# Delta-rule layers of a hybrid network: the inverse of a 32-token triangle in full, then one solution step

## The reference, cut to what matters

```python
def step(W, inp):
    qt, kt, vt, bt = inp
    wk = jnp.einsum('bhde,bhe->bhd', W, kt)
    v_new = bt * (vt - wk)
    W = W + jnp.einsum('bhd,bhe->bhde', v_new, kt)
    out = jnp.einsum('bhde,bhe->bhd', W, qt)
    return (W, out)
# q, k = softmax over 32; beta = sigmoid; the input is a layer norm's output times slow_w
```

## Time and profile before

| | us |
|---|---|
| three runs, median (lowest, highest) | 5387.88 (5385.71, 5416.66) |
| the profiled execution | 5345.09 |
| its span, first to last instruction | 5343.3 |
| first delta-rule stage, start of M's scaling in chunk 0 to chunk 31 | 392.9 to 1194.3 |
| second delta-rule stage, the same | 1638.8 to 2453.3 |

### The profile page before, as it was taken

The page is one execution under the profiler, slowest core; times in us unless marked ns, Lnnn a source line. Parts: engine busy times, 40 slices in busy tenths (PEclk is TensorE's granted clock), DMA queues, the critical chain, the costliest instruction groups (busy, mean ns, idle before and its releaser), DMA issues. The chain is left out here.

```text
span 5343.3 us, 141254 instructions
## 1 busy us (share of the span) xinstructions
PE 4536.1 (85%) x57740; PEld 2868.5 (54%) x57741; DVE 2973.0 (56%) x5849; ACT 2153.1 (40%) x4123; POOL 853.9 (16%) x2139
## 2 busy tenths in 40 slices
PE   3678888888988988998777987799999999985995
PEld 1247777773437777774354654345454455443663
DVE  3445444453024444454577887488685885864343
ACT  1123232332123333231365566177575775741221
POOL 0000000000000000000454555011111111102112
PEclk7779888898988888798888988899999999996997
DMA  1000000000000000000100000000000000005223
GB/s 42 2 7 3 3 3 3 3 3 18 0 6 3 3 3 3 3 3 3 38 1 1 1 1 1 10 1 0 1 0 1 1 0 1 0 3 194 87 85 100
DMA packets 47557, 85.79 MB, mean 16 GB/s; under 512 B 7120, under 2 KB 38128, under 8 KB 46064
## 3 DMA queue, kind: packets, MB, share of 16 engines
q1 hardware_dynamic: 40944, 61.84, 3.4%
q0 software_dynamic: 6144, 16.79, 1.0%
HBM read 45.05 MB, written 33.55 MB: 15 GB/s over the span
## 5 line engine op out<-in xcount | busy, mean ns | idle before, releaser
L1769 PE MATMUL psum<-hm_ex,hm_mix 128*128 128x512 f32 x1024 | 510.9, 622 | 42.1 <-ACT hm_Aq L1849 38.1
L1835 ACT ACTIVATE hm_ex<-psum,hm_nm 128x1024 f32<-128x1024 f32 x256 | 285.5, 1115 | 300.6 <-DVE hm_nm L1893 300.6
L1769 PEld LDWEIGHTS psum<-hm_ex,hm_mix 128*128 128x128 f32 x1024 | 175.7, 191 | 353.1 <-issue 345.4
L1908 DVE COPY hm_A<-psum 128x1024 f32<-128x1024 f32 x256 | 312.9, 1222 | 51.5 <-PE psum L1778 47.8
L1903 DVE TENSOR_SCALAR_CACHE_REDUCE hm_plus<-hm_Aq,hm_cbcol,hm_sums 128x1024 f32<-128x1024 f32 x256 | 340.5, 1330 | 0.0
L1893 DVE TENSOR_REDUCE hm_nm<-psum 128x1 f32<-128x1024 f32 x256 | 311.1, 1215 | 14.5 <-PE psum L1757 14.5
L1778 PEld LDWEIGHTS psum<-K,hm_Aq 128*128 128x128 f32 x2048 | 236.7, 140 | 149.9 <-issue 145.2
L957 DVE TENSOR_TENSOR fw_M<-fw_M,psum 128x256 f32<-128x256 f32 x256 | 107.9, 421 | 344.9 <-PE psum L728 342.4
L1307 ACT ACTIVATE pt_signs<-pt_acts,pt_tb 128x1024 f32<-128x1024 f32 (+1 forms) x224 | 227.8, 1020 | 146.7 <-POOL pt_tb L1180 104.4
L1840 ACT ACTIVATE hm_junk<-hm_Aq 128x1024 f32<-128x1024 f32 x256 | 270.6, 1057 | 30.3
L1757 PE MATMUL psum<-hm_kt,hm_qd 64*32 64x512 f32 x4096 | 280.9, 607 | 0.0
(11 more groups left out here) (380 smaller groups left out, 9117.4 us busy)
## 6 DMA issues: line engine op xcount, KB each, us to landing
ex_rows_in<-ex_zero SPq DMA_DIRECT2D x2, 5120.0 KB, 24.8
ex_xs<-ex_rows_in SPq DMA_DIRECT2D x80, 128.0 KB, 2.0
ex_rows_out<-ex_ys SPq DMA_DIRECT2D x80, 128.0 KB, 1.7
ex_w<-in_ex_w SPq DMA_DIRECT2D x2, 4096.0 KB, 23.0
X<-in_x SPq DMA_DIRECT2D x2, 2048.0 KB, 12.5
out_y<-X SPq DMA_DIRECT2D x2, 2048.0 KB, 9.0
ff_w<-in_ff_w SPq DMA_DIRECT2D x2, 1024.0 KB, 5.9
pt_w_proc<-in_pt_proc SPq DMA_DIRECT2D x1, 2048.0 KB, 7.6
```

The source lines that it names most:

```text
L1769: mm = pe.matmul(bank[4 + c], mix[:, u, :], ex[:, u, 512 * c:512 * c + 512], start=True, stop=True)
L1835: act.activation(ex[:, u, :], flat2(psum[:, 2 * u:2 * u + 2, :]), ACT.Exp, bias=nm[:, u:u + 1], accum_out=rsum[:, u:u + 1]).then_inc(s_ex, 1)
L1908: dve.tensor_copy(A[:, :, :, QT_ * t:QT_ * t + QT_], flat2(psum[:, 6:8, :]).rearrange("p (m g n) -> p m g n", m=MT, g=HEADS)).then_inc(s_a ...
```

## The change

The inverse of the 32 x 32 triangle is made in full by small-tile products, and one solve with it takes the place of four. With nn = -N and nn' = -N^T (both are now made), nn^2 by a product, nz = nn z3 by another, S = 1 + nn + nn^2 on VectorE (`series`), S nz by a third, and inv = z3 + S nz (`inverse`). TensorE calls product ten times for a chunk: l8, z1, z2, tt as before; zt (the transpose of z3, as a product with the identity), and two for N and N^T, in a row behind turn; two (nb) for nn^2 and nn z3 behind gram 0; one (nc) for S nz behind through_state 1. One solve(sa) is left, behind through_state 2. VectorE's two additions `solution` become `series` (two operations of 256 columns) and `inverse` (one); `solved` now copies where it added, and stands ahead of softmax. ScalarE no longer copies r0 (512 columns) and spreads one matrix, invx, in place of two; it copies nz, zn (256 columns each) and nn (512). GpSimd clears one wide matrix in place of two.

```diff
@@ tensor
-                def product(left, right):
+                def product(b, at, left, right, sig):
                     for n in range(HEADS):
-                        for b in range(4):
-                            mm = pe.matmul(bank[5][rows(b), DH * n:DH * n + DH], right[rows(b), n, :], left[rows(b), n, :],
-                                           start=True, stop=True)
-                    mm.then_inc(s_t, 1)
-
-                def solve(by, of, sig):
+                        for c in range(4):
+                            mm = pe.matmul(bank[b][rows(c), at + DH * n:at + DH * n + DH], right[rows(c), n, :],
+                                           left(rows(c), n), start=True, stop=True)
+                    mm.then_inc(sig, 1)
...
+                def solve(a):
                     for n in range(HEADS):
-                        mm = pe.matmul(bank[2][:, 64 * n:64 * n + 64], by[:, n, :], of(n), start=True, stop=True)
-                    mm.then_inc(sig, 1)
+                        hd = DH * (2 * (n % 4) + n // 4)
+                        mm = pe.matmul(bank[2][:, 64 * n:64 * n + 64], invx[:, n, :], rhs[:, a % 2, :, hd:hd + DH],
+                                       start=True, stop=True)
+                    mm.then_inc(s_ap, 1)
...
-                    if so:
-                        pe.wait_ge(s_zx, s + 1)
-                        solve(z3x, given, s_y)
                     if ch:
                         pe.wait_ge(s_trc, i + 1)
                         pe.sem_inc(s_go, 1)
                         gram(a, 0, s_ga)
+                    if so:
+                        pe.wait_ge(s_nn, s + 1)
+                        pe.wait_ge(s_zn, s + 1)
+                        pe.sem_inc(s_go, 1)
+                        product(5, 0, of(nn[:, 0]), nn[:, 1], s_nb)
+                        product(2, C, of(zn), nn[:, 0], s_nb)
...
-                    if so:
-                        pe.wait_ge(s_nt, s + 1)
-                        pe.wait_ge(s_r0, s + 1)
-                        solve(ntx, first, s_ap)
                     if rc:
                         pe.wait_ge(s_m, r * 5 + 2)
                         through_state(ra, 1)
+                    if so:
+                        pe.wait_ge(s_s1, s + 1)
+                        pe.wait_ge(s_nz, s + 1)
+                        pe.sem_inc(s_go, 1)
+                        product(2, 0, of(s1), nz, s_nc)
...
-                    if so:
-                        pe.wait_ge(s_rk, s * 2 + 1)
-                        solve(ntx, later, s_ap)
...
                         through_state(ra, 2)
+                    if so:
+                        pe.wait_ge(s_ix, s + 1)
+                        solve(sa)
...
-                    if so:
-                        pe.wait_ge(s_rk, s * 2 + 2)
-                        solve(ntx, later, s_ap)
...
+                    if nxt:
+                        turn(i + 1, (a + 1) % 4)
                     if ch:
                         pe.wait_ge(s_z, i * 2 + 2)
                         pe.wait_ge(s_lo, i + 1)
                         pe.sem_inc(s_go, 1)
-                        product(z3, loff)
-                    if nxt:
-                        turn(i + 1, (a + 1) % 4)
+                        product(2, 0, one, z3, s_zt)
+                        product(5, 0, of(z3), loff, s_na)
+                        product(5, C, of(loff), z3, s_na)
@@ scalar
                     if so:
-                        act.wait_ge(s_y, s + 1)
+                        act.wait_ge(s_nb, s * 2 + 2)
+                        act.activation(flat(nz[:, :, :]), bank[2][:, C:2 * C], ACT.Copy).then_inc(s_nz, 1)
...
+                    if so:
+                        act.wait_ge(s_inv, s + 1)
                         if since(s, 1):
-                            act.wait_ge(s_pu, s)
-                        act.activation(r0[:, :, :, :].rearrange("p n y e -> p (n y e)"), bank[2], ACT.Copy).then_inc(s_r0, 1)
+                            act.wait_ge(s_ap, s)
+                        spread(invx, inv, 1.0, s_ix)
...
-                    if ch:
-                        act.wait_ge(s_z, i * 2 + 2)
-                        spread(z3x, z3, 1.0, s_zx)
-                        act.wait_ge(s_t, i * 5 + 5)
-                        spread(ntx, bank[5][:, 0:C].rearrange("p (h j) -> p h j", j=DH), -1.0, s_nt)
...
+                    if ch:
+                        act.wait_ge(s_zt, i + 1)
+                        act.activation(flat(zn[:, :, :]), bank[2][:, 0:C], ACT.Copy).then_inc(s_zn, 1)
+                        act.wait_ge(s_na, i * 2 + 2)
+                        act.activation(nn[:, :, :, :].rearrange("p y h j -> p (y h j)"), bank[5], ACT.Copy,
+                                       scale=-1.0).then_inc(s_nn, 1)
@@ vector
-                def solution(s, it):
-                    dve.wait_ge(s_ap, s * 3 + it + 1)
-                    dve.tensor_tensor(rk[:, :, :, :].rearrange("p n y e -> p (n y e)"), bank[2],
-                                      r0[:, :, :, :].rearrange("p n y e -> p (n y e)"), ALU.add).then_inc(s_rk, 1)
+                def series(s):
+
+                    dve.wait_ge(s_nb, s * 2 + 1)
+                    own.done(dve.tensor_tensor(s1[:, :, :], result(5), nn[:, 0], ALU.add))
+                    dve.tensor_tensor(s1[:, :, :], s1[:, :, :], small(2, HEADS), ALU.add).then_inc(s_s1, 1)
+
+                def inverse(s):
+                    dve.wait_ge(s_nc, s + 1)
+                    if since(s, 1):
+                        dve.wait_ge(s_ix, s)
+                    dve.tensor_tensor(inv[:, :, :], result(2), z3[:, :, :], ALU.add).then_inc(s_inv, 1)
...
```

More of the change, by code:

```diff
@@ L601, in fast_weight_stage @@
         compact = lambda n: sb(n, [P, HEADS, DH])
[L602 to L605, removed]
+        l8, l8t, bg, loff, qm, z1, z2, tt, z3, l2, zn, nz, s1, inv = (
+            compact(n) for n in "l8 l8t bg loff qm z1 z2 tt z3 l2 zn nz s1 inv".split())
+        nn = sb("nn", [P, 2, HEADS, DH])
+        invx = sb("invx", [P, HEADS, P])
         pu = sb("pu", [P, 2, C]); pk = sb("pk", [P, C]); pkt = sb("pkt", [P, 2, C])
@@ L610, in fast_weight_stage @@
         M = sb("M", [P, 2, P])
[L611 to L612 removed]
+        names = ("w zero staged proj dif exp qk tr trc ga gb bg l8 qm lo in t l2 tt z na zt nn zn nb s1 nz nc inv ix "
+                 "ap pu pt ptc ra u rm m intra fin go dch").split()
         (s_w, s_zero, s_staged, s_proj, s_dif, s_exp, s_qk, s_tr, s_trc, s_ga, s_gb, s_bg, s_l8, s_qm, s_lo, s_in,
[L614 removed]
+         s_t, s_l2, s_tt, s_z, s_na, s_zt, s_nn, s_zn, s_nb, s_s1, s_nz, s_nc, s_inv, s_ix, s_ap, s_pu, s_pt, s_ptc,
          s_ra, s_u, s_rm, s_m, s_intra, s_fin, s_go, s_dch) = (k.sem(f"s_{n_}_{n}") for n in names)
@@ L653, in body @@
                         if since(i, 1):
-                            pool.wait_ge(s_t, i * 5)
+                            pool.wait_ge(s_na, i * 2)
                         pool.tensor_tensor(loff[:, :, :], bg[:, :, :], off, ALU.mult).then_inc(s_lo, 1)
-                for to in (z3x, ntx):
-                    pool.memset(to[:, :, :], 0.0).then_inc(s_zero, 1)
+                pool.memset(invx[:, :, :], 0.0).then_inc(s_zero, 1)
                 for a in range(4):
@@ L775, in body @@
                         pe.sem_inc(s_go, 1)
-                        product(l8, l8t)
+                        product(5, 0, of(l8), l8t, s_t)
                     if rc:
@@ L790, in body @@
                         pe.sem_inc(s_go, 1)
-                        product(z1, l2)
+                        product(5, 0, of(z1), l2, s_t)
                     if rc:
@@ L797, in body @@
                         pe.sem_inc(s_go, 1)
-                        product(z2, l2)
+                        product(5, 0, of(z2), l2, s_t)
                     if rc:
@@ L808, in body @@
                         pe.sem_inc(s_go, 1)
-                        product(tt, l2)
+                        product(5, 0, of(tt), l2, s_t)
                     if rc:
@@ L859, in body @@
                     if ch:
-                        act.wait_ge(s_t, i * 5 + 3)
+                        act.wait_ge(s_t, i * 4 + 3)
                         act.activation(flat(tt[:, :, :]), bank[5][:, 0:C], ACT.Copy).then_inc(s_tt, 1)
@@ L886, in _ @@
                 k.load_table(act, ACT.Exp)
-                act.wait_ge(s_zero, 6)
+                act.wait_ge(s_zero, 5)
                 k.credit(act, s_fin, 1)
@@ L969, in solved @@
                     got = bank[2].rearrange("p (b m y e) -> p b m y e", b=2, m=4, y=2)
-                    was = r0[:, :, :, :].rearrange("p (b m) y e -> p b m y e", b=2)
                     for n, to in enumerate((pu[:, a % 2, :], pk[:, :])):
-                        own.mark(dve.tensor_tensor(to.rearrange("p (m b e) -> p b m e", m=4, b=2),
-                                                   got[:, :, :, n, :], was[:, :, :, n, :], ALU.add))
+                        own.mark(dve.tensor_copy(to.rearrange("p (m b e) -> p b m e", m=4, b=2), got[:, :, :, n, :]))
```

(16 more changed lines are left out.)

16 lines of the change are left out of this document (7 added, 9 removed).

## The result

The changed kernel takes 5739.31 us (median of 4 runs, 5733.02 to 5749.65), the kernel before 5396.8 (5385.71 to 5416.66) in the same job, that is, among the runs made together with it: ratio 1.0637, 95% interval 1.0598 to 1.0675. It is slower by 342 us; the forecast was +262, inside its range.

The account below looks back on a forecast made before the run. TensorE's list bounds the kernel now; after the change, instruction packet delivery would. Chunk 27.8 plus clock 2.5 gives 30.3 us a step against 26.06, +262 us over 62 steps, so 5650 us from 5387.88; range 5430 to 5870.

Parts of the forecast that it names:

- Rival A: TensorE's instruction supply: several packets fetched at once under steady demand, so delivery keeps pace; 5310 us, chance 0.12.
- B: TensorE's instruction supply: short only now and then, 1 us of stalls a chunk; 5400 us, no difference, chance 0.10.
- C: TensorE's granted clock in the stages: it does not come back; 5950 us, chance 0.10.
- chunks at full clock of 26 to 28 us: Sign expected in the profile after: how long chunks of the two stages take at full clock.
- The work, -2.3 us: TensorE's work a chunk: three solves go, -6.0 us, five products come, +3.7; net -2.3 us.
- The walk, 21.9 us against 22.4: Engines' lists through one chunk, full clock, instructions at will: 21.9 us against 22.4, two new waits included.
- 25.6 of delivery: Instruction packets a chunk: 1792 records are 7.5 packets, 25.6 us at 3.4 each, the chunk's new floor.
- 1.5 of pauses: During project and the solve, few records are used and delivery pauses: 1.5 us a chunk (0.8 to 2).
- 0.7 for the jump: Loop's jump back: stays at 3.5 us, six times in 31 steps, 0.7 us a step.
- 2.5 for the clock: TensorE's granted clock in the stages: costs 2.5 us a step, taken between 1.6 (as now) and 3.7.
- The upper value for the clock, 3.7: Upper end of the clock's cost in the stages: 3.7 us a step, half of the way to 35.
- the densest 14 us hold well over 1000 records: Sign against the forecast in TensorE's densest stretch; before the change no more than 985 were found in 14 us.

Follow-up runs that it names:

- e1: Changed kernel with six second-level products as 128-column matmuls, 1216 records a chunk, values altered: stages 1548.8 us against 1968.8; whole 9643.26 us on another path.
- e2: Kernel before with each of its five products issued twice in 32-column matmuls, +640 records a chunk: 5914.55 us, ratio 1.1073.
- e3: Kernel before with each of its five products' columns streamed once more in 128-column matmuls, +160 records a chunk: 5425.99 us, ratio 1.0159.
- e4: Changed kernel with four idle 512-column matmuls added a chunk, 16 records in all: 5732.29 us, ratio 1.0732.
- e8: e6 with the pair moved behind gram 1, nc behind with_state 1, and series and inverse later on VectorE: 5282.16 us, ratio 0.9874.
- e6: e5 with the two nb products also paired into one of 64 columns a matmul, 1408 records a chunk: 5376.77 us, ratio 0.9966.
- e5: Changed kernel without zt and the second na product, VectorE transposing z3 and nn instead, 1536 records a chunk: 5498.71 us, ratio 1.0197.
- e7: Changed kernel with only the two nb products moved, behind with_state 0 and gram 1, same records: 5704.27 us, ratio 1.065.
- e10: Kernel before with its three solves on ntx for one head only, values altered: stages 1637.6 us against 1615.9; whole 9772.39 us on another path.

## Why the prediction was right, and where its terms were off

*The bound.* It said that the chunk's floor becomes the delivery of instructions, 7.5 packets, and that taking work off does not lower it. Measured: 7.5 packets a chunk in the loop, 7.26 a step over a stage, and steps of 31.05 and 32.46 us against 30.3. e1 shows that without the extra records the loss is gone, e2 against e3 that records slow the kernel before as well, at equal columns, and the packets' times that the pauses end when one has landed. Rival A (delivery keeps pace, 5310) falls with e1; B (short now and then, 5400) with 5.2 us of "issue" a step. C (the clock does not come back, 5950) is not wholly gone: its number is off by 210 us, and a clock that never came back would be granted at 0.5 and not at 0.71 and 0.68, but no chunk ran at full clock, where the kernel before had 29 that did. For the same reason the sign "chunks at full clock of 26 to 28 us" could not be read.

*The work, -2.3 us.* The prices held at full clock: a product 0.74, the solve 2.00; and a copy out of PSUM in `solved` takes 0.42 (0.41 was taken), as do the operations of `series` and `inverse` (418 to 425 ns). Not all of VectorE's operations of 256 columns do: M's scaling (L1005) takes 0.35, two in `lower` 0.53 (L950) and 0.84 (L951). Busy time nonetheless rose by 0.65 us a step, as it was done at 0.71 and 0.68 in place of 0.89 and 0.85.

*The walk, 21.9 us against 22.4.* Both new waits came: l8 by up to 1.2 us (22 times, mean 0.7 where 1.2 was forecast), turn by up to 1.2, 27 times, mean 1.2 where 0.9 was forecast. With instructions at will the order would have gained 0.5 us a step by the walk; e1, the nearest to that, gains 1.1, and its wait for l8 is 1.4 in the mean (42.5 us in 30).

*The sum of the instruction terms.* Here the size failed. 25.6 of delivery, 1.5 of pauses, 0.7 for the jump and 2.5 for the clock were 30.3. With 7.26 packets the first is 24.7 at 3.4 us each, the jump is right (19.7 us over 7, 0.6 a step), and the measured mean of 31.8 leaves 6.4 for pauses and clock together, where 4.0 was forecast. The price of 3.4 us was that of the closest packets: in the first stage a twentieth of their distances are at or below 3.4 us, half are at or above 3.97, and the mean is 4.28 (962.5 over 225), with up to 8.2 us where TensorE uses few records. At 3.97 the delivery alone would be 28.8 us, so a good part of the 6.4 may be the packet's price and not pauses. The upper value for the clock, 3.7, came from a chunk of 35 us at a granted 0.50, an estimate of mine that no run shows, and so the 2.5 is not shown either; the one chunk of the changed kernel that had 0.50 throughout (2767.4 to 2797.3, behind the loop) took 29.9 us. How the 6.4 divide between price, pauses and clock is open; e4 moved work and clock together and does not separate them. The forecast erred on the low side, 80 us of 342, by this term.

*A sign that I had named and that spoke falsely.* "Wrong if the densest 14 us hold well over 1000 records": they hold 1200. But they stand behind 7.6 us of project, z1, through_state and solve, with 190 records, and inside them TensorE stops for 1.94 us for instructions, until 458.10. Four packets of some 238 records start within the 14 us, but the last of them, at 463.10, lands at 464.13, behind its end. With three landed some 490 records stood ready. The reserve was about two packets, where I had assumed about one, and a window as short as 14 us measures reserve and delivery together. The chunk, 1792 records in 31.1 us, is the window that shows the delivery.

## What to carry over

Count the instructions of an engine's list for each stretch of time, as its busy time is counted, and set them against the packets of the instruction queue; idle time that ended in "issue" inside a group which waits for nothing was the sign here that it was short ("issue" was 5.2 us a step after, 1.6 before). In this kernel TensorE could take some 1400 records in 25 us (e8, 1408 in 25.2); beyond that each cost 15.5 to 17 ns, so a small matmul and its load, two records, cost 31 to 34 ns where they take 11.6 ns of TensorE's time (0.74 us for 64). The cure was fewer and wider instructions for the same arithmetic (e1, 25.0 us a step; e6, 26.2), or another engine's (e5, 27.9), and not the order (e7, 31.8); with the list at 1408 the order counted again (e8, 25.2 against e6's 26.2).

## What the runs showed of the hardware that I had not expected

- More work raised the granted clock and cost next to nothing: e4, 0.71 to 0.84 in the first stage for 3.4 us more of matmuls in a chunk; step +0.55 us. Some 1.5 us of the 3.4 came back through the clock.
- Less work lowered it and gained nothing: e10, 0.89 to 0.75 for 5.2 us less, step +0.35 us.
- VectorE transposes 8 heads in 32 x 32 blocks, 128 x 256 values, in about 0.44 us, whether from PSUM or from SBUF (e6; the copies out of PSUM in the changed kernel take 0.42). A product with the identity costs TensorE 0.74 us, 128 records, and a copy on ScalarE of 0.39 (L889 in the changed kernel):

```profile
L983 DVE STREAM_TRANSPOSE fw_wt<-fw_w 128x256 f32<-128x256 f32 x31 | 13.8, 445 | 4.7 <-DVE fw_qm L957 4.2
L978 DVE STREAM_TRANSPOSE fw_t<-psum 128x256 f32<-128x256 f32 x31 | 13.6, 440 | 0.0
```
